# Two additions of a mixing MLP in pieces of one node tile, and another order for the last edge group of a graph layer

## The chip, the cores and the metric

The kernel runs on one core of a Trainium2 chip. The metric is the time of one execution on the device, in microseconds (us). Before the change three runs took 3339.9, 3343.6 and 3344.3 us; their median is 3343.6 us.

In the profile PE is TensorE's matmul part and PEld its weight load, DVE is VectorE, ACT is ScalarE, POOL is GpSimd, SP is SyncE. ACTq and SPq are the queues on which ACT and SP issue DMAs.

## What is computed

One layer over 12,500 nodes of 256 features and 212,500 edges sorted by their destination: a graph attention, a linear attention with an MLP over all nodes (the mixing), and a mixture of experts.

```python
xn = _layernorm(x)
# graph attention, 8 heads of 32
h  = einsum('ni,hif->hnf', xn, W)
ea = leaky(s_src[:, src] + s_dst[:, dst]).T
ea = exp(ea - segment_max(ea, dst)[dst])
ea = ea / (segment_sum(ea, dst)[dst] + EPS)
gnn = segment_sum(hn[src] * ea[:, :, None], dst)      # 12500 x 256
# mixing
y = xn + attention(xn)
h = _layernorm(y, norm_g, norm_b)
mix = y + gelu(h @ w_fc1 + b_fc1) @ w_fc2 + b_fc2
x = x + gnn + mix
return x + ffn(_layernorm(x))                          # top 2 of 8 experts
```

## The kernel before

It is written with one instruction stream for each engine and semaphores between them, in three stages with a barrier between: the node stage (a table with h and the scores of each node is written to HBM), the edge stage, and the stage of routing and experts. The change lies in the edge stage.

**Edges.** 128 edges are a chunk and 16 chunks (`CB`) a group; there are 104 groups (`GROUPS`), the last of them number 103. 212,500 edges fill 1661 chunks; the other three of the 1664 hold padding. For each chunk `edges_pool` issues one indirect DMA on POOL (L1215) that gathers 128 rows of the table into a column of `rows`, by indices that it finds in the SBUF tile `srcix`. `rows` has three buffers (`NR`), so the gather of a chunk waits until the sum of the chunk three groups earlier is made.

A group k then passes through these steps, which the text calls by their functions:

- `copy_scores` (ACT, L1309) waits for all 16 gathers of the group and copies the score columns; `turn_scores` (PE, L1261 and L1262) transposes them into bank 0.
- `breaks` and `edge_scores` (DVE, L1372 to L1409) make the maximum of each segment by scans along the row; `exp_scores` (ACT, L1315) takes the exponential; `turn_weights` (PE, L1268 and L1269) and `copy_weights` (ACT, L1320) turn the result back.
- `one_hot` (DVE, L1381 and L1384) compares each edge's fragment number with a ramp; it makes the matrix that sums the edges of one destination. It needs nothing of the gather. It reads the ramp from bank 0, into which `turn_scores` writes other columns, so the two take turns.
- `weigh` (DVE, L1416, four quarters of a group) multiplies the rows by the weights; `sums` (PE, L1279, four quarters of four chunks, two matmul passes for each chunk) adds up; `copy_sums` (ACT, L1329, a copy for each chunk) moves the sum out of one of three banks. After a group's 16 copies ACT issues two DMAs that store them (L1349, L1351).

The order is written out by hand. On PE `turn_scores(k + 1)` stands ahead of all of `sums(k)`, and `turn_weights(k + 1)` between its second and third quarter. On ACT `exp_scores(k + 1)` and `copy_weights(k + 1)` stand amid `copy_sums(k)`, and `copy_scores(k + 2)` behind it. On DVE `one_hot(k + 1)` stands behind `edge_scores(k + 1)`.

**Beside the edges** run the mixing MLP (in groups up to 91) and most of a merge of fragments across chunks (groups 92 to 101): `Beside` hands out their steps by the count of its calls, four in a group, whatever the time is. `mlp_vector` treats the nodes in 25 supernodes of four tiles of 128 nodes (`SUPERS`; the last has two). Two of its instructions in each supernode add one SBUF tile to another, both 128 partitions by 1024 values: L1154 adds the bias `mb2` to `m_xs`, and L1137 in `ended` adds `m_xs` to the result `m_x2`. The last window of the merge follows the last edge group, then comes the barrier.

Of the kernel before, what the change touches and what calls it, by code (L numbers as in the profile page):

```python
# [33 lines left out]
BLOCKS = -(-GROUPS * CB // P)  # L34
CHUNKS = BLOCKS * P
NEAR = 32
FAR = CHUNKS * NEAR
# [15 lines left out]
NR = 3  # L53
# [1037 lines left out]
def mlp_vector(v, vec, S, B):  # L1091
# [41 lines left out]
    def ended(k):  # L1133
        if k >= 0:
            x2, n = B.m_x2[k % 2], SUPERS[k][1]
            v.wait_ge(S.m_y, pairs_to(k))
            v.tensor_tensor(x2[:, 0:n, :], x2[:, 0:n, :], B.m_xs[:, 0:n, :], ALU.add).then_inc(S.m_x3, 1)  # L1137

# [5 lines left out]
    for k, (s, n) in enumerate(SUPERS):  # L1144
        free = mlp_banks(k)[2]
        added(k - 1, 1)
        yield
        ended(k - 1)
        yield
        yield from idle(3)  # L1150
        attended(k + 1, 0, free)
        yield
        v.wait_ge(S.m_xs, 16 * (k + 1))
        vec(v.tensor_tensor(B.m_xs[:, 0:n, :], B.m_xs[:, 0:n, :], B.mb2[:, :].unsqueeze(1).to_broadcast([P, n, D]), ALU.add))  # L1154
        v.wait_ge(vec.sem, vec.n)
        yield
        yield from idle(2)
        attended(k + 1, 1, free)
        yield
        yield from norm(k + 1)  # L1160
        added(k, 0)
        yield
# [45 lines left out]
def edges_pool(p, S, B, groups):  # L1208
    for k in groups:
        b = k % NR  # L1210
        for j in range(CB):
            col = k * CB + j
            if k >= NR:
                p.wait_ge(S.sum, (k - NR) * CB + j + 1)
            p.indirect_dma_start(out=B.rows[b][:, j, :], out_offset=None, in_=B.table[:, :],  # L1215
                                 in_offset=bass.IndirectOffsetOnAxis(ap=B.srcix[:, col:col + 1], axis=0)).then_inc(S.rows_in[b], 16)
# [37 lines left out]
def edges_tensor(pe, S, B):  # L1254
    beside = Beside(mix_tensor(pe, S, B), mlp_tensor(pe, S, B), merge_tensor(pe, S, B))

    def turn_scores(k):
        pe.wait_ge(S.sce, k + 1)
        pe.wait_ge(S.oh, 2 * k)
        pe.wait_ge(S.inb, k)  # L1260
# [23 lines left out]
    for k in range(GROUPS):  # L1284
        more = k + 1 < GROUPS
        if more:
            turn_scores(k + 1)
        sums(k, 0)
        beside()
        sums(k, 1)  # L1290
        beside()
        if more:
            turn_weights(k + 1)
        sums(k, 2)
        beside()
        sums(k, 3)
        beside()
    for _ in beside.steps:
# [3 lines left out]
def edges_scalar(a, S, B):  # L1302
    beside = Beside(mix_scalar(a, S, B), mlp_scalar(a, S, B), merge_scalar(a, S, B))

    def copy_scores(k):
        r, b = k % NR, k % 2
        a.wait_ge(S.rows_in[r], 16 * CB * (k // NR + 1))
        a.wait_ge(S.tsc, max(k - 1, 0))
# [26 lines left out]
    for k in range(GROUPS):  # L1335
        more = k + 1 < GROUPS
        copy_sums(k, 0)
        beside()
        copy_sums(k, 1)
        if more:  # L1340
            exp_scores(k + 1)
        beside()
        if more:
            copy_weights(k + 1)
        copy_sums(k, 2)
        beside()
        copy_sums(k, 3)
        a.wait_ge(S.ev, CB * (k + 1))
        a.dma_start(B.frag[k * CB * NEAR:(k + 1) * CB * NEAR, :].rearrange("(c l) f -> l c f", l=NEAR),  # L1349
                    B.fout[k % 2][0:NEAR, :, :]).then_inc(S.near[k % 2], 16)  # L1350
        a.dma_start(B.last_d[k * CB:(k + 1) * CB, :], B.fout[k % 2][P - 1:P, :, :]).then_inc(S.near[k % 2], 16)  # L1351
        if k + 2 < GROUPS:
            copy_scores(k + 2)
# [9 lines left out]
def edges_vector(v, vec, S, B):  # L1363
# [13 lines left out]
    def one_hot(k):  # L1377
        b = k % 2
        v.wait_ge(S.inb, k + 1)
        v.wait_ge(S.sum, max(CB * (k - 1), 0))  # L1380
# [42 lines left out]
    for k in range(GROUPS):  # L1423
        more = k + 1 < GROUPS
        weigh(k, 2)
        weigh(k, 3)
        if more:
            breaks(k + 1)
            edge_scores(k + 1)
        beside()  # L1430
        if more:
            one_hot(k + 1)
# [952 lines left out]
```

## Time and profile before

| | |
|---|---|
| three runs | 3339.9, 3343.6, 3344.3 us |
| span of the profiled execution, first to last instruction | 3339.0 us |
| POOL busy over the span | 2259.8 us (68%) |
| gathers L1215 | 1664 of 971 ns in the mean, from 153.7 us to 2275.8 us |
| last edge group's last copy | 2300.8 us |
| first instruction behind the barrier | 2317.3 us |

For the profiled execution no time besides its span is given; the runs lie 0.9 to 5.3 us above that span, their median 4.6 us.

How to read it. A busy share over the whole span mixes three stages. For the edge stage the useful views are those that give, for one engine, the duration of each instruction and the idle time ahead of it. An engine whose instructions follow one another with the same short pause all the way is paced by itself; one that waits for others shows pauses of all lengths. Where the durations of equal instructions differ, the timeline shows what ran beside the long ones. At the end of a stage the timeline alone tells which wait ended last.

### The profile page before, as it was taken

How to read it: one execution, taken by the hardware profiler on the slowest of the kernel's cores; microseconds unless marked ns; L12 is line 12 of the kernel's file. 1: busy time of each engine (PE TensorE's matmuls, PEld its weight loads, DVE VectorE, ACT ScalarE, POOL GpSimd, SP SyncE). 2: the span in 40 equal slices, each digit the busy share in tenths (PEclk: the TensorE clock that was granted, in tenths of full speed). 3: DMA queues.
4: the chain of work that ended last, by engine and by line, in shares of the span. 5: the costliest groups of instructions: out<-in, count | busy, mean ns of one | idle time of the engine just before them, and what ended most of it. 6: DMA issues, size and time to landing. Idle time of an engine off the chain costs nothing.

```text
span 3339.0 us, 42310 instructions
## 1 busy us (share of the span) xinstructions
PE 2671.4 (80%) x11566; PEld 2083.1 (62%) x11566; DVE 2000.5 (60%) x5275; ACT 1555.4 (47%) x3383; POOL 2259.8 (68%) x2203
## 2 busy tenths in 40 slices
PE   8657767888888888888898886564289998899997
PEld 6545555665666666566665664443168787778886
DVE  7445566776777767677676766775546456454221
ACT  5335543554554554455555454333245554444442
POOL 0277777777777777777777777773646677666444
PEclk9879988999999999999999998777589999999998
DMA  8797765665666665666566666555756666666552
GB/s 274 249 288 196 203 178 164 170 174 162 171 177 168 180 166 167 179 168 176 160 169 175 167 168 162 163 154 136 265 132 156 163 160 147 142 135 140 99 90 44
DMA packets 399353, 562.41 MB, mean 168 GB/s; under 512 B 72761, under 2 KB 319567, under 8 KB 398938
## 3 DMA queue, kind: packets, MB, share of 16 engines
q0 software_dynamic: 124848, 299.04, 34.8%
q1 hardware_dynamic: 197033, 171.49, 17.6%
q10 hardware_dynamic: 77161, 88.52, 10.2%
q8 instruction: 99, 1.62, 0.2%
q14 instruction: 212, 1.74, 0.2%
HBM read 403.67 MB, written 170.61 MB: 172 GB/s over the span
## 4 chain that ended last, share of the span: by engine, by line
PE 55%; DMA 14%; POOL 11%; issue 8%; ACT 8%; DVE 4%; ACTq 1%; POOLq 0%; SPq 0%; DVEq 0%
PE bank L1279 21%; DMA rows<-table,srcix 9%; PE bank L1082 7%; PE bank L2169 6%; PE bank L2182 6%; POOL rows L1215 5%; PE bank L1071 4%; DMA out<-x_y,x_dest 3%; POOL sorted_d L1708 3%; POOL out L2254 2%; PE bank L1044 2%; PE bank L592 1%; PE bank L593 1%; PE bank L852 1%; ACT L1315 1%
## 5 line engine op out<-in xcount | busy, mean ns | idle before, releaser
L1215 POOL DMA_INDIRECT rows<-table,srcix x1664 | 1615.2, 971 | 507.3 <-issue 353.9
L1279 PE MATMUL bank<-rows,onehot 128*128 128x272 f32 x3328 | 931.9, 428 | 56.0 <-ACT fout L1329 52.5
L1329 ACT ACTIVATE fout<-bank 128x272 f32<-128x272 f32 x1664 | 641.0, 397 | 577.3 <-PE bank L1279 532.3
L1279 PEld LDWEIGHTS bank<-rows,onehot 128*128 128x128 f32 x3328 | 668.9, 208 | 243.7 <-ACT fout L1329 78.7
L1416 DVE TENSOR_TENSOR rows<-rows,bank 128x1024 f32<-128x1024 f32 x416 | 483.9, 1212 | 183.6 <-ACT rows L1320 183.2
L2254 POOL DMA_INDIRECT out<-x_y,x_dest x210 | 336.7, 1603 | 296.6 <-DMA out<-x_y,x_dest 168.8
L2169 PE MATMUL bank<-x_int,x_w1c 128*128 128x256 f32 x1680 | 392.8, 388 | 18.8 <-ACT x_w1c L2198 9.5
L2182 PE MATMUL bank<-e_w,x_ht 128*128 x1680 | 390.6, 387 | 11.7 <-DVE x_y L2235 8.6
L2169 PEld LDWEIGHTS bank<-x_int,x_w1c 128*128 128x128 f32 x1680 | 326.0, 195 | 68.7 <-issue 22.6
L2182 PEld LDWEIGHTS bank<-e_w,x_ht 128*128 128x128 f32 x1680 | 317.7, 194 | 56.8 <-issue 16.0
L2207 ACT ACTIVATE x_ht<-bank,x_b1c 128x256 f32<-128x256 f32 x420 | 174.4, 471 | 376.6 <-PE bank L2169 376.4
L1071 PE MATMUL bank<-m_hnt,fc_w 128*128 128x512 f32 (+1 forms) x600 | 283.9, 598 | 28.9 <-ACT m_hid L1183 28.9
L1261 PE MATMUL bank<-ident,sc_e 128*128 128x128 f32 x104 | 39.1, 376 | 296.4 <-ACT sc_e L1309 287.5
L1082 PE MATMUL bank<-fc_w,m_hid 128*128 128x256 f32 x1176 | 270.8, 382 | 0.0
L1389 DVE SCALAR_TENSOR_TENSOR g_sdm<-notself,bank 128x128 f32<-128x128 f32 x104 | 29.9, 288 | 387.7 <-PE bank L1262 387.3
L1309 ACT ACTIVATE sc_e<-rows 128x256 f32<-128x256 f32 x104 | 43.3, 416 | 449.7 <-DMA rows<-table,srcix 430.6
L1082 PEld LDWEIGHTS bank<-fc_w,m_hid 128*128 128x128 f32 x1176 | 226.3, 192 | 34.4
L1708 POOL DMA_INDIRECT sorted_d<-e_hn,e_row x196 | 193.5, 987 | 64.9 <-issue 53.9
L1381 DVE TENSOR_TENSOR onehot<-bank,loc 128x2032 f32<-128x2032 f32 x104 | 235.6, 2265 | 0.2
L1261 PEld LDWEIGHTS bank<-ident,sc_e 128*128 128x128 f32 x104 | 16.7, 161 | 337.6 <-ACT sc_e L1309 327.1
L1071 PEld LDWEIGHTS bank<-m_hnt,fc_w 128*128 128x128 f32 x600 | 117.1, 197 | 122.9 <-issue 73.8
L2235 DVE TENSOR_TENSOR x_y<-bank,x_b2c 128x512 f32<-128x512 f32 x105 | 72.3, 689 | 184.8 <-PE bank L2182 184.7
(375 smaller groups left out, 3233.4 us busy)
## 6 DMA issues: line engine op xcount, KB each, us to landing
frag<-fout ACTq DMA_DIRECT2D x104, 544.0 KB
x_in<-sorted_d SPq DMA_DIRECT2D x105, 260.0 KB
rows<-table,srcix POOLq DMA_INDIRECT x1664
x_b2c<-in_L_ffn_b SPq DMA_DIRECT2D x105, 128.0 KB, 3.6
frag<-in_x ACTq DMA_DIRECT2D x1, 13416.0 KB
table<-hr SPq DMA_DIRECT2D x24, 544.0 KB, 4.1
xs<-in_x SPq DMA_DIRECT2D x24, 512.0 KB, 6.0
xg<-in_x SPq DMA_DIRECT2D x24, 512.0 KB, 6.3
```

The costliest lines, as they stand in the source:

```text
L1071: t = pe.matmul(bank[own[m % 2]][:, 0:n * P], B.mw1[:, kk, m * P:(m + 1) * P], B.m_hnt[:, kk, 0:n * P], start=(kk == 0), stop=(kk == KD - 1))
L1082: t = pe.matmul(bank[own[i // 2]][:, i % 2 * D:(i % 2 + 1) * D], B.m_hid[:, m, i * P:(i + 1) * P], B.mw2[:, m, :], start=(m == 0), stop=(m ...
L1215: p.indirect_dma_start(out=B.rows[b][:, j, :], out_offset=None, in_=B.table[:, :], in_offset=bass.IndirectOffsetOnAxis(ap=B.srcix[:, col:c ...
L1279: pe.matmul(B.banks[2 + c % 3][:, 0:ROW], B.onehot[k % 2][:, j, :], B.rows[k % NR][:, j, :], start=True, stop=True).then_inc(S.sum, 1)
L1329: a.activation(B.fout[k % 2][:, j, :], B.banks[2 + c % 3][:, 0:ROW], ACT.Copy).then_inc(S.ev, 1)
L1381: v.tensor_tensor(B.onehot[b][:, :, 0:P - 1], B.banks[0][:, 2 * P:3 * P - 1].unsqueeze(1).to_broadcast([P, CB, P - 1]), B.loc[:, k * CB:(k ...
L1416: v.tensor_tensor(h, h, w.unsqueeze(3).to_broadcast([P, n, GH, GF]), ALU.mult).then_inc(S.wgh, 1)
L1708: p.indirect_dma_start(out=B.sorted_d[:, :], out_offset=bass.IndirectOffsetOnAxis(ap=B.e_row[:, j, at:at + 1], axis=0), in_=B.e_hn[r % NH] ...
L2169: t = pe.matmul(out, B.w1c[u][:, k, m * P:(m + 1) * P], B.gt[u][:, k, :], start=(k == 0), stop=(k == KD - 1))
L2182: t = pe.matmul(bk[BANKS_OUT[u]][:, i * D:(i + 1) * D], B.ht[u][:, m, i * P:(i + 1) * P], B.w2[:, bass.ds(ex * HT + m, 1), :], start=(m == ...
L2207: a.activation(B.ht[u][:, m, :], B.banks[BANKS_H[m * 2 // HT]][:, m % 2 * ET:(m % 2 + 1) * ET], ACT.Gelu, bias=B.b1c[w][:, m:m + 1]).then_ ...
L2254: p.indirect_dma_start(out=B.out[:, :], out_offset=bass.IndirectOffsetOnAxis(ap=B.dest[j % (NOUT + 1)][:, i:i + 1], axis=0), in_=B.y[j % N ...
```

## The change

Three things are changed.

1. The two additions in `mlp_vector` are made a node tile at a time: four instructions of 128 by 256 in place of one of 128 by 1024. In `ended` the last of the four waits until the others are complete, since it alone raises the semaphore `m_x3` that lets the result be stored.
2. The three chunks of padding are not gathered: `edges_pool` issues 1661 gathers, and `copy_scores` of the last group waits for 13.
3. In the iteration of group 102 the work for group 103 is put in another place. On PE `turn_scores(103)` goes behind three quarters of `sums(102)`, and `turn_weights(103)` behind the fourth. On ACT `copy_scores(103)` goes behind two quarters of `copy_sums(102)`, and `exp_scores(103)` and `copy_weights(103)` behind all of it. On DVE `one_hot(103)` goes ahead of `breaks(103)` and `edge_scores(103)`; `turn_scores(103)` now waits for it.

```diff
 def ended(k):
-            v.tensor_tensor(x2[:, 0:n, :], x2[:, 0:n, :], B.m_xs[:, 0:n, :], ALU.add).then_inc(S.m_x3, 1)
+            for i in range(n - 1):
+                vec(v.tensor_tensor(x2[:, i, :], x2[:, i, :], B.m_xs[:, i, :], ALU.add))
+            v.wait_ge(vec.sem, vec.n)
+            v.tensor_tensor(x2[:, n - 1, :], x2[:, n - 1, :], B.m_xs[:, n - 1, :], ALU.add).then_inc(S.m_x3, 1)
...
-        vec(v.tensor_tensor(B.m_xs[:, 0:n, :], B.m_xs[:, 0:n, :], B.mb2[:, :].unsqueeze(1).to_broadcast([P, n, D]), ALU.add))
+        for i in range(n):
+            vec(v.tensor_tensor(B.m_xs[:, i, :], B.m_xs[:, i, :], B.mb2[:, :], ALU.add))
...
 def edges_pool(p, S, B, groups):
-        for j in range(CB):
+        for j in range(min(CB, REAL - k * CB)):          # REAL = -(-N_EDGES // P) = 1661
...
 def edges_tensor: turn_scores(k)
-        pe.wait_ge(S.oh, 2 * k)
+        pe.wait_ge(S.oh, 2 * k + (2 if k == GROUPS - 1 else 0))
 def edges_tensor: the loop
-        more = k + 1 < GROUPS
-        if more:
+        more, early = k + 1 < GROUPS, k + 2 < GROUPS
+        if early:
             turn_scores(k + 1)
         sums(k, 0)
         sums(k, 1)
-        if more:
+        if early:
             turn_weights(k + 1)
         sums(k, 2)
+        if more and not early:
+            turn_scores(k + 1)
         sums(k, 3)
+        if more and not early:
+            turn_weights(k + 1)
 def edges_scalar: copy_scores(k), and the loop
-        a.wait_ge(S.rows_in[r], 16 * CB * (k // NR + 1))
+        a.wait_ge(S.rows_in[r], 16 * (CB * (k // NR) + min(CB, REAL - k * CB)))
...
         copy_sums(k, 1)
-        if more:
+        if early:
             exp_scores(k + 1)
-        if more:
+        if early:
             copy_weights(k + 1)
+        elif more:
+            copy_scores(k + 1)
         copy_sums(k, 2)
         copy_sums(k, 3)
+        if more and not early:
+            exp_scores(k + 1)
+            copy_weights(k + 1)
...
-        if k + 2 < GROUPS:
+        if k + 3 < GROUPS:
             copy_scores(k + 2)
 def edges_vector: one_hot(k), and the loop
-        v.wait_ge(S.inb, k + 1)
+        v.wait_ge(S.inb, min(k + 1, GROUPS - 1))
...
         weigh(k, 3)
+        if more and not early:
+            one_hot(k + 1)
         if more:
             breaks(k + 1)
             edge_scores(k + 1)
-        if more:
+        if early:
             one_hot(k + 1)
```

On DVE in the MLP, at the first supernode, before: `m_x<-m_x,m_xs` is the addition of L1137, between the scores and the one-hot of an edge group.

```order
L1409 TENSOR_TENSOR g_fm<-g_d,neq 128x128
L1137 TENSOR_TENSOR m_x<-m_x,m_xs 128x1024
L1381 TENSOR_TENSOR onehot<-bank,loc 128x16x127
L1384 CAST onehot<-islast 128x16
```

The same place in the changed kernel:

```order
L1423 TENSOR_TENSOR g_fm<-g_d,neq 128x128
L1139 TENSOR_TENSOR m_x<-m_x,m_xs 128x256 x3
L1141 TENSOR_TENSOR m_x<-m_x,m_xs 128x256
L1395 TENSOR_TENSOR onehot<-bank,loc 128x16x127
```

One row became four instructions at the same place of the stream; nothing around it moved.

On ACT at the last edge groups, before. The rows begin with eight copies of group 101; `sc_e<-rows` is `copy_scores(103)`, `g_w<-g_ea` is `exp_scores(103)`, `rows<-bank` is `copy_weights(103)`.

```order
L1329 ACTIVATE fout<-bank 128x272 x8
L1349 DMA frag<-fout 32x16x272
L1351 DMA last_d<-fout 1x4352
L1309 ACTIVATE sc_e<-rows 128x256
L1329 ACTIVATE fout<-bank 128x272 x8
L1315 ACTIVATE g_w<-g_ea 128x128
L1320 ACTIVATE rows<-bank 128x2x16x8
L1329 ACTIVATE fout<-bank 128x272 x8
```

Changed:

```order
L1363 DMA frag<-fout 32x16x272
L1365 DMA last_d<-fout 1x4352
L1338 ACTIVATE fout<-bank 128x272 x8
L1318 ACTIVATE sc_e<-rows 128x256
L1338 ACTIVATE fout<-bank 128x272 x8
L1324 ACTIVATE g_w<-g_ea 128x128
L1329 ACTIVATE rows<-bank 128x2x16x8
L1363 DMA frag<-fout 32x16x272
L1365 DMA last_d<-fout 1x4352
L1338 ACTIVATE fout<-bank 128x272 x16
```

All 16 copies of group 102 are now ahead of `exp_scores(103)`, eight of them ahead of `copy_scores(103)`.

On PE at the same place, before: the first two rows are `turn_scores(103)`, `bank<-ident,g_w` and `bank<-ident,g_fm` are `turn_weights(103)`; `bank<-rows,onehot` are sums, where the listing counts one for each chunk and pass.

```order
L1261 MATMUL bank<-ident,sc_e 128x128
L1262 MATMUL bank<-ident,sc_e 128x128
L1279 MATMUL bank<-rows,onehot 128x272 x8
L1268 MATMUL bank<-ident,g_w 128x128
L1269 MATMUL bank<-ident,g_fm 128x128
L1279 MATMUL bank<-rows,onehot 128x272 x24
```

Changed:

```order
L1284 MATMUL bank<-rows,onehot 128x272 x20
L1266 MATMUL bank<-ident,sc_e 128x128
L1267 MATMUL bank<-ident,sc_e 128x128
L1284 MATMUL bank<-rows,onehot 128x272 x4
L1273 MATMUL bank<-ident,g_w 128x128
L1274 MATMUL bank<-ident,g_fm 128x128
L1284 MATMUL bank<-rows,onehot 128x272 x16
```

The x20 are eight chunks of group 101 and twelve of group 102, which stood behind `turn_scores(103)` before.

## Rows read from the trace of the kernel before

**Rows 1.** The page: the chain that ended last, by engine and by line.

```profile
PE 55%; DMA 14%; POOL 11%; issue 8%; ACT 8%; DVE 4%; ACTq 1%; POOLq 0%; SPq 0%; DVEq 0%
```

**Rows 2.** The page's groups: count, then busy us and mean ns, then idle before.

```profile
L1215 POOL DMA_INDIRECT rows<-table,srcix x1664 | 1615.2, 971 | 507.3 <-issue 353.9
```

**Rows 3.** Instructions of L1215: duration min/median/max in ns, first and last start.

```profile
L1215 POOL DMA_INDIRECT rows<-table,srcix x1664: 942/949/1970, 153.7 to 2274.8; - x185
```

**Rows 4.** Stretches: length, busy us (count) of PE, PEld, DVE, ACT, POOL; PEclk, DMA, GB/s.

```profile
588.00:2045.00 1457.00, 1244.59 (x4895) 911.94 (x4893) 1018.90 (x2188) 758.57 (x1661) 1109.27 (x1141) 0.94 0.61 170
```

**Rows 5.** Instructions of L1137 and of L1154, as in rows 3.

```profile
L1137 DVE TENSOR_TENSOR m_x<-m_x,m_xs x25: 685/1219/1258, 623.9 to 2042.0; 128x1024 f32<-128x1024 f32 x24, 128x512 f32<-128x512 f32 x1
L1154 DVE TENSOR_TENSOR m_xs<-m_xs,fc_b x25: 685/1216/1221, 588.2 to 2004.0; 128x1024 f32<-128x1024 f32 x24, 128x512 f32<-128x512 f32 x1
```

**Rows 6.** Timeline, two places: start, us, engine, line; idle before in brackets.

```profile
623.94 1.22 DVE L1137 TENSOR_TENSOR m_x<-m_x,m_xs 128x1024 f32<-128x1024 f32 x1
...
624.56 1.42 POOL L1215 DMA_INDIRECT rows<-table,srcix  x1 [0.30 <-PE bank L1279]
...
1054.53 1.21 DVE L1154 TENSOR_TENSOR m_xs<-m_xs,fc_b 128x1024 f32<-128x1024 f32 x1
1054.61 1.95 POOL L1215 DMA_INDIRECT rows<-table,srcix  x1 [0.30 <-issue]
```

**Rows 7.** Timeline, in the merge: two additions or products follow each other on DVE.

```profile
2111.01 1.23 DVE L1591 TENSOR_TENSOR mg_last<-mg_last,mg_cbeta 128x1024 f32<-128x1024 f32 x1 [6.24 <-ACT mg_cbeta L1521]
2111.16 1.90 POOL L1215 DMA_INDIRECT rows<-table,srcix  x1 [0.30 <-issue]
2112.15 0.18 DVE L1592 TENSOR_TENSOR mg_last<-mg_last,mg_cbeta 128x32 f32<-128x32 f32 x1
```

**Rows 8.** Instructions of L523 in the node stage, and their timeline.

```profile
L523 DVE TENSOR_TENSOR ix_hot_lo<-wcat,avec x4: 415/416/417, 12.1 to 13.1; 128x256 f32<-128x256 f32 x4
...
12.13 1.42 DVE L523 TENSOR_TENSOR ix_hot_lo<-wcat,avec 128x256 f32<-128x256 f32 x4
```

**Rows 9.** Timeline, the last edge groups (102 and 103).

```profile
2271.17 3.52 ACT L1329 ACTIVATE fout<-bank 128x272 f32<-128x272 f32 x8 [0.17 <-SPq L1248]
...
2272.13 4.60 DVE L1416 TENSOR_TENSOR rows<-rows,bank 128x1024 f32<-128x1024 f32 x4
...
2274.84 0.95 POOL L1215 DMA_INDIRECT rows<-table,srcix  x1 [0.30 <-issue]
...
2275.10 0.36 ACTq L1351 DMA_DIRECT2D last_d<-fout  x1
...
2280.92 0.42 ACT L1309 ACTIVATE sc_e<-rows 128x256 f32<-128x256 f32 x1 [6.22 <-DMA rows<-table,srcix]
...
2281.39 0.48 PE L1261 MATMUL bank<-ident,sc_e 128*128 128x128 f32 x1 [7.13 <-ACT sc_e L1309]
...
2282.19 0.29 DVE L1389 SCALAR_TENSOR_TENSOR g_sdm<-notself,bank 128x128 f32<-128x128 f32 x1 [4.79 <-PE bank L1262]
...
2284.84 0.40 ACT L1329 ACTIVATE fout<-bank 128x272 f32<-128x272 f32 x1 [0.51 <-PE bank L1279]
...
2285.46 0.28 DVE L1409 TENSOR_TENSOR g_fm<-g_d,neq 128x128 f32<-128x128 f32 x1
...
2285.66 2.27 DVE L1381 TENSOR_TENSOR onehot<-bank,loc 128x2032 f32<-128x2032 f32 x1
...
2287.85 0.30 ACT L1315 ACTIVATE g_w<-g_ea 128x128 f32<-128x128 f32 x1
...
2289.10 4.61 DVE L1416 TENSOR_TENSOR rows<-rows,bank 128x1024 f32<-128x1024 f32 x4 [1.08 <-ACT rows L1320]
...
2293.64 0.97 ACT L1329 ACTIVATE fout<-bank 128x272 f32<-128x272 f32 x3 [0.88 <-PE bank L1279]
...
2294.85 5.90 ACT L1329 ACTIVATE fout<-bank 128x272 f32<-128x272 f32 x13 [0.24 <-PE bank L1279]
```

**Rows 10.** A stretch of that end, columns as in rows 4.

```profile
2281.40:2286.00 4.60, 4.60 (x13) 3.60 (x14) 3.54 (x12) 1.47 (x4) 0.00 (x0) 0.55 0.00 0
```

More of the change, by code:

```diff
@@ L35 @@
 CHUNKS = BLOCKS * P
+REAL = -(-N_EDGES // P)
 NEAR = 32
@@ L1335, in edges_scalar @@
     for k in range(GROUPS):
-        more = k + 1 < GROUPS
+        more, early = k + 1 < GROUPS, k + 2 < GROUPS
         copy_sums(k, 0)
@@ L1423, in edges_vector @@
     for k in range(GROUPS):
-        more = k + 1 < GROUPS
+        more, early = k + 1 < GROUPS, k + 2 < GROUPS
         weigh(k, 2)
         weigh(k, 3)
+        if more and not early:
+            one_hot(k + 1)
         if more:
```

## The prediction

> **What bounds the kernel now.** I read four views in this order: the chain that ended last, the page's groups, the instructions of the gather line L1215, and the timeline where its durations differ. The chain names TensorE first (55%) and POOL with 11% [rows 1]. That does not settle it: the chain goes back through whatever released each step, and inside an edge group it runs through TensorE even when the group as a whole came late. The gathers tell more. Their 1664 instructions have 507.3 us of idle time ahead of them [rows 2], which is 0.305 us each, and the timeline shows 0.30 wherever one looks [rows 6, 7, 9]. Half of the instructions take 949 ns or less [rows 3]. So POOL issues one gather each 0.949 + 0.305 = 1.254 us from 153.7 to 2275.8 us and waits for nobody: **the edge stage is paced by POOL**, 1664 x 1.254 = 2086.7 us. TensorE is busy 1244.6 of 1457 us beside the MLP, 85%, and DVE 70% [rows 4]: near, but not full.
>
> The stage lasts longer than 2086.7 us because some gathers take up to 1970 ns [rows 3]. The groups have 1615.2 us busy [rows 2], and 1664 x 0.949 = 1579.1, so stalls inside gathers cost 36.1 us. What stalls them is in the timeline. A gather that starts 0.08 us behind an L1154 lasts 1.95 us, one that starts 0.62 us behind an L1137 lasts 1.42 us [rows 6]. Both end 0.82 us after the DVE instruction ends (1054.53 + 1.21 = 1055.74, the gather at 1056.56; 625.16 and 625.98). An undisturbed gather would have 0.82 us left at 0.949 - 0.82 = 0.13 us past its start. So it asks for something 0.13 us in, and it gets it only when the DVE instruction is over. I followed this for all 50 instructions of the two lines: 1.22 us each [rows 5], and the gathers that ask while they run lose 9.7 us at L1137 and 11.3 us at L1154, together **21.0 us of the 36.1**.
>
> The Trainium skill (SBUF — State Buffer, section Who interferes with whom) has the reason: a VectorE instruction with two SBUF inputs takes a read port that it shares with GpSimd, for its whole length, and blocks a GpSimd instruction that reads SBUF. The trace agrees: the stalls end with the DVE instruction, and the gather reads its indices from `srcix`.
>
> **Part 1: the additions in four pieces.** Let a gather start s after the DVE instruction. In the trace it is stalled for s from about 0.05 us on, by 1.09 - s (1.01 for the 0.08 above, 0.47 for the 0.62). Gathers start every 1.254 us, at any phase, so one instruction costs on average (1.09 - 0.05)^2 / 2 / 1.254 = 0.43 us; 50 of them 21.5, where the trace has 21.0. Now the pieces. A 128x256 product of two SBUF tiles takes 0.416 us, and four in a row 1.42 us [rows 8], one each 0.335. A gather that asks in a piece's time waits until the end of that piece, if POOL is served between two pieces: (0.416 - 0.13 - 0.05)^2 / 2 / 1.254 = 0.022 us for each of 196 pieces (98 node tiles, twice), 4.4 us. Putting the pieces at the 50 recorded places, with the gathers at their recorded phases, gives 5.2 us. I take 5.2, the one with this kernel's phases: **-15.8 us**.
>
> Is POOL served in between? In the merge L1592, also with two SBUF inputs, starts at 2112.15, before L1591 ends at 2112.24; the gather between them ends at 2113.06, which is 0.82 behind L1591 and not 0.82 behind L1592's 2112.33 [rows 7]. All the places of this kind that I found in the merge read so. They are few, which keeps the other answer alive (below). The bounds of this part: no stall left, -21.0; POOL never served inside a chain, the replay gives 33.0 us of stalls, +12.0.
>
> DVE has more to do: (1.42 - 1.22) for L1154, and some 0.3 for L1137, whose last piece waits for the three ahead; 25 x 0.5 = 12.5 us on an engine that is 70% busy [rows 4]. Behind L1137 stand `one_hot` and `weigh`, and PE waits for those; a group comes 0.3 us later in one group of three. No gather waits for it, since none waits for a sum now. I cost it at nothing; without that cover it would be up to 12.5 us.
>
> **Parts 2 and 3: the end of the edge stage.** Three gathers fewer are 3 x 1.254 = 3.8 us on POOL. What becomes of that is decided by the chain behind it, which I follow in the times of rows 9. *Before:* the last gather starts at 2274.84, its data lets `copy_scores(103)` start at 2280.92. Meanwhile PE stands still, for 7.1 us, though group 102's rows were weighted by 2276.7: its sums are queued behind `turn_scores(103)`. They then run at half clock, 1.2 GHz (0.55 granted in that stretch [rows 10]); `exp_scores(103)` waits for eight of their copies until 2287.85, though the scores were ready at 2285.5; `weigh(103)` starts at 2289.10, the first copy of group 103 at 2293.64, and the last is over at 2300.76.
>
> *After:* PE goes on with group 102 as soon as group 101 is summed (its last copy is over at 2274.7), and ACT, free of its DMA issues at 2275.5, makes eight copies (8 in 3.52 us [rows 9]) until 2279.0. By then the 13 gathers have landed (2280.9 - 3.8 = 2277.1), so ACT copies the scores at 2279.0 to 2279.5. PE has to end the third quarter, whose last chunk needs a bank that ACT frees at 2279.9, so the transposes run at about 2280.4. `one_hot(103)`, 2.3 us on DVE behind `weigh(102)`, is over at 2279.1 and `breaks(103)` at 2279.9, ahead of it. `edge_scores(103)` starts at 2281.0, takes its 3.55 us (2282.19 to 2285.74 [rows 9]) to 2284.6, with the difference that `exp_scores` reads ready at 2284.4. ACT has ended group 102 near 2283.5 and starts at once; 1.25 us from there to `weigh(103)` as before (2287.85 to 2289.10) gives 2285.6. One quarter of weighing, 1.2, and a sum later the first copy is at 2287.4. Sixteen copies took 2300.76 - 2293.64 = 7.1 us; the last ends at 2294.5: **6.2 us earlier**, padding included. The two DMA issues of group 102 (0.8 us on ACT, now behind `copy_weights(103)`) lie under `weigh(103)`. With the 3.8 us alone, in the old order, it would be 3.8.
>
> Against it stands the clock. PE has only two transposes to do from about 2283.3 to 2286.8. Before, after 7.1 us with nothing, it was granted half (0.55) for the first 4 us of work, in which a chunk takes 0.9 us instead of 0.44 (the copy at 2284.84 lasts 0.40 and had waited 0.51 for PE [rows 9]). If that comes back, 4 us hold 4.4 chunks instead of 9.1, a loss of 2.1 us. The gap is shorter than the old one, so I take half of it, 1.0, and have **-5.2 us**, between -4.1 and -6.2. If neither the padding nor the reordering brings anything, this part is 0.
>
> **Sum.** -15.8 - 5.2 = -21.0. The profiled span 3339.0 becomes 3318.0. The runs' median lies 4.6 us above that span, so the time is 3343.6 - 21.0 = **3322.6 us**. Everything behind the barrier starts earlier and stays as it is.
>
> **Rivals.**
> *A, slower: POOL is not served inside a chain of pieces.* For it: each piece starts 0.08 us before its predecessor's recorded end (0.335 against 0.416 [rows 8]), so the next may hold the port already, and the witnesses [rows 7] are followed by much shorter instructions. Against it: those same rows. Price: stalls last up to 1.42 us, the replay gives 23.6 us if the wait ahead of L1137's last piece lets POOL in and 33.0 if not, for 21.0 now. With the end's -5.2 the time is 3341.0 to 3350.4. It turns slower than before where a chain stalls by over 26.2 us in all.
> *B: what stalls the gathers is not these instructions but something that comes with them, so their length does not matter.* Then only the end of the stage is left, 3343.6 - 5.2 = 3338.4. Against it: durations of 1.95, 1.42 and 1.90 us, each 0.82 us past the end of a `tensor_tensor` [rows 6, 7]. The same page and section of the Trainium skill says that a `tensor_tensor` was not seen to stall DMAs, and infers that writing descriptors needs only the write port; by that the first part would bring nothing, and the rows disagree.
> *C: something behind POOL takes the gain.* PE at 85% and DVE at 70% of a stretch that gets 1% shorter have room; only if the chain of a group were already as long as three groups of gathers would a gather begin to wait for a sum. The idle time of 0.305 everywhere speaks against it. If half of the first part went this way: 3330.5.
> That the change does not do what it says is excluded by the order of instructions shown above.
>
> **Chances.** Forecast 0.78, A 0.07, B 0.05, C 0.10. The forecast's own range is 3343.6 less 16 to 25 us, and 2 us of scatter on either side for the three runs (they lie 4.4 us apart): 3317 to 3330. Up to 3331 it takes in part of C; A and B stay outside. About what a measurement can tell from no change is 0.2%, 6.7 us: below 3336.9 is faster, above 3350.3 slower. Faster: 0.78 and most of C, 0.86. Within: B, half of A, a little of C, 0.11. Slower: 0.03, the far end of A.
>
> **What the new profile would show.** The gather's maximum falls from 1970 ns; its mean from 971 to about 961; all gathers together 1661 x 0.949 + 20.3 = about 1597 us busy, and the idle time stays 0.305 each (507). A gather near one of the pieces is stalled by at most 0.24 us. The last gather starts near 2255 (2274.8 - 15.8 - 3.8). No idle time of 7 us on PE behind it; from the last gather's start to the end of the last copy 25.9 us become about 24.5. If gathers beside the pieces last 1.6 us and more, A is right; if idle times over 0.4 us appear ahead of them, C. The prediction is wrong also if the last copies come 0.9 us apart throughout (the clock), which costs 7 us.

## The result and the profile after

| | before | after |
|---|---|---|
| median of eight runs each | 3343.5 us | 3324.3 us |
| all runs | 3337.3 to 3355.8 | 3320.7 to 3330.5 |
| span of the profiled execution | 3339.0 | 3320.5 |
| start of the 1661st gather (the last that holds edges) | 2271.1 | 2256.3 |
| from there to the end of the last copy of group 103 | 29.7 | 25.1 |
| from there to the end of the program | 1038.2 | 1039.1 |

The ratio is 0.9945, with a 95% interval from 0.9931 to 0.996: 18 us faster, between 13 and 23. The forecast was 3322.6 us, in a range from 3317 to 3330, or to 3331 with a part of rival C.

The page of the changed kernel: the first line is the chain that ended last by engine, the second the group of the gathers (L1215 is L1220 now).

```profile
PE 56%; DMA 13%; POOL 9%; ACT 8%; issue 7%; DVE 6%; ACTq 1%; SPq 0%; POOLq 0%; DVEq 0%
...
L1220 POOL DMA_INDIRECT rows<-table,srcix x1661 | 1598.0, 962 | 506.1 <-issue 357.7
```

Against [rows 1, 2] the gathers are busy 17.2 us less, 2.8 of it the three that are gone, and the idle time ahead of each is still 0.305 us (506.1 / 1661). So POOL still paces the stage and waits for nobody; the chain's shares hardly tell it, as before.

The instructions of that line and of the additions: duration min/median/max in ns, first and last start.

```profile
L1220 POOL DMA_INDIRECT rows<-table,srcix x1661: 942/947/1982, 153.5 to 2256.3; - x185
...
L1139 DVE TENSOR_TENSOR m_x<-m_x,m_xs x73: 408/417/452, 627.6 to 2029.0; 128x256 f32<-128x256 f32 x73
...
L1141 DVE TENSOR_TENSOR m_x<-m_x,m_xs x25: 424/425/466, 628.7 to 2029.4; 128x256 f32<-128x256 f32 x25
...
L1159 DVE TENSOR_TENSOR m_xs<-m_xs,fc_b x98: 409/417/479, 585.2 to 1992.1; 128x256 f32<-128x256 f32 x98
```

For [rows 5] there are 196 pieces of 0.42 us where 50 instructions of 1.22 us stood. The maximum of the gathers did not fall (1982 ns for the 1970 of [rows 3]): the four longest that are left, 1.77 to 1.98 us, lie in the merge.

The timeline at two additions, DVE and POOL, as [rows 6]:

```profile
1112.74 1.42 DVE L1159 TENSOR_TENSOR m_xs<-m_xs,fc_b 128x256 f32<-128x256 f32 x4
1113.40 1.58 POOL L1220 DMA_INDIRECT rows<-table,srcix  x1 [0.30 <-PE bank L1284]
...
1444.52 1.08 DVE L1139 TENSOR_TENSOR m_x<-m_x,m_xs 128x256 f32<-128x256 f32 x3
1445.01 1.08 POOL L1220 DMA_INDIRECT rows<-table,srcix  x1 [0.30 <-PE bank L1284]
1445.64 0.42 DVE L1141 TENSOR_TENSOR m_x<-m_x,m_xs 128x256 f32<-128x256 f32 x1
```

The lower gather asks at 1445.01 + 0.13 = 1445.14, in the second piece (1444.86 to 1445.27), and ends at 1446.09, 0.82 us behind that piece: stalled by 0.13 us. The upper one asks at 1113.53, in the third piece, which ends at 1113.83. It ends at 1114.98, 0.82 us behind the *fourth* piece (1114.16), and is stalled by 0.63 us, where at most 0.24 was forecast. Both kinds matter below.

Where the 18.5 us between the spans come from: 14.8 from the stretch up to the 1661st gather, 4.6 from the end of the stage, and 0.9 are lost behind it, which is less than the same stretch differs between other kernels below. Of the 14.8, gathers beside the additions lose 7.6 us instead of 21.0 (13.4), gathers elsewhere 14.1 instead of 15.0 (0.9); the other 0.5 are an earlier first gather (0.2) and idle time (0.3).

The end of the stage, where [rows 9] stood: the sums of group 102, then `copy_scores(103)`, `edge_scores(103)` from its first to its last instruction, `exp_scores(103)`, `weigh(103)`, and the copies of group 103.

```profile
2255.66 5.21 PE L1284 MATMUL bank<-rows,onehot 128*128 128x272 f32 x22
...
2261.89 2.27 DVE L1395 TENSOR_TENSOR onehot<-bank,loc 128x2032 f32<-128x2032 f32 x1
...
2264.16 0.41 ACT L1318 ACTIVATE sc_e<-rows 128x256 f32<-128x256 f32 x1
...
2265.99 0.29 DVE L1403 SCALAR_TENSOR_TENSOR g_sdm<-notself,bank 128x128 f32<-128x128 f32 x1 [1.10 <-PE bank L1267]
...
2269.26 0.28 DVE L1423 TENSOR_TENSOR g_fm<-g_d,neq 128x128 f32<-128x128 f32 x1
2269.37 0.31 ACT L1324 ACTIVATE g_w<-g_ea 128x128 f32<-128x128 f32 x1 [1.22 <-DVE g_ea L1421]
...
2270.63 4.61 DVE L1430 TENSOR_TENSOR rows<-rows,bank 128x1024 f32<-128x1024 f32 x4 [1.09 <-ACT rows L1329]
...
2273.29 0.40 ACT L1338 ACTIVATE fout<-bank 128x272 f32<-128x272 f32 x1 [2.70 <-PE bank L1284]
...
2275.03 6.37 ACT L1338 ACTIVATE fout<-bank 128x272 f32<-128x272 f32 x14 [0.51 <-PE bank L1284]
```

PE no longer stands still for 7.1 us behind the last gather; the exponential starts 0.03 us after the scores are ready instead of 2.3 us.

### The profile page after: what moved, and what is told of

It is laid out like the page before. It is cut to its first block, busy times and chain, and to the rows that moved or that the text cites. A ratio compares the mean times of both kernels' runs of the same rounds, so it can differ in the third digit from the quotient of the medians.

```text
span 3320.5 us, 42453 instructions
## 1 busy us (share of the span) xinstructions
PE 2669.9 (80%) x11566; PEld 2081.3 (63%) x11566; DVE 2013.9 (61%) x5421; ACT 1554.9 (47%) x3383; POOL 2242.3 (68%) x2200
## 4 chain that ended last, share of the span: by engine, by line
PE 56%; DMA 13%; POOL 9%; ACT 8%; issue 7%; DVE 6%; ACTq 1%; SPq 0%; POOLq 0%; DVEq 0%
PE bank L1284 21%; DMA rows<-table,srcix 9%; PE bank L1083 7%; PE bank L2185 6%; PE bank L2198 6%; PE bank L1072 5%; POOL rows L1220 5%; DMA out<-x_y,x_dest 2%; POOL sorted_d L1724 2%; PE bank L1045 2%; PE bank L593 1%; PE bank L594 1%; PE bank L853 1%; POOL out L2270 1%; ACT L1324 1%
## 5 line engine op out<-in xcount | busy, mean ns | idle before, releaser
L1220 POOL DMA_INDIRECT rows<-table,srcix x1661 | 1598.0, 962 | 506.1 <-issue 357.7
```

## The experiments

All numbers of a run's profile below are from one execution. "Time" is the median of a kernel's executions, their number in brackets, and behind it the median of the kernel before in the same comparison. "Stalls" is what gathers last beyond 0.949 us; "beside the additions" are those that start while one of the two additions runs. "End" is the time from the start of the 1661st gather to the end of the last copy. Kernels that gather the padding start their last gather 3.8 us behind the 1661st.

| kernel | time, before | last gather starts | all stalls | beside the additions | end |
|---|---|---|---|---|---|
| before | 3343.5 (8) | 2274.8 | 36.0 | 21.0 | 29.7 |
| after | 3324.3 (8), 3343.5 | 2256.3 | 21.7 | 7.6 | 25.1 |
| pieces_only | 3329.8 (6), 3346.7 | 2257.1 | 19.1 | 8.1 | 29.6 |
| end_only | 3343.2 (12), 3346.7 | 2276.9 | 42.1 | 27.3 | 25.3 |
| halves | 3331.5 (1), 3346.7 | 2263.3 | 24.1 | 10.9 | 28.4 |
| one_input | 3327.2 (1), 3346.7 | 2262.9 | 25.1 | 9.2 | 29.8 |
| one_input_slow | 3331.8 (1), 3339.1 | 2263.3 | 25.5 | 8.6 | 29.8 |
| waits_between | 3322.4 (1), 3339.1 | 2250.5 | 16.7 | 4.9 | 26.4 |
| eighths | 3328.3 (1), 3339.1 | 2264.0 | 28.7 | 16.2 | 25.7 |
| merge_too | 3320.2 (6), 3339.1 | 2251.8 | 17.6 | 6.2 | 27.8 |

### Each part alone

`pieces_only` is the kernel before with the lines of the diff in `mlp_vector`, and nothing else:

```diff
+            for i in range(n - 1):
+                vec(v.tensor_tensor(x2[:, i, :], x2[:, i, :], B.m_xs[:, i, :], ALU.add))
...
+        for i in range(n):
+            vec(v.tensor_tensor(B.m_xs[:, i, :], B.m_xs[:, i, :], B.mb2[:, :], ALU.add))
```

> The kernel before with the two additions in pieces of one node tile, and nothing else of the change. Port theory (a gather is stalled only until the end of the two-input DVE instruction that runs when it asks, and POOL paces the stage): the last gather starts 13 to 16 us earlier than 2274.8, the gathers' busy time falls from 1615 to about 1601 us, from the last gather's start to the end of the last copy it stays near 26 us, time 3328 to 3330. Rival A (POOL not served inside a chain): the last gather starts later than 2274.8 by 3 to 12 us, 3346 to 3355. Rival C (something behind POOL takes it): gathers stall less, but idle times over 0.4 us appear ahead of them and the time is above 3335.

Measured: the ratio to the kernel before is 0.9951 (0.9935 to 0.9968), median 3329.8 us where the kernel before has 3346.7 in the same comparison. The last gather starts at 2257.1, 17.7 us earlier, a little more than expected: 12.9 of it are stalls beside the additions, 4.0 stalls elsewhere, which the change does not touch; without those it would be 13.7. The end takes 29.6 us, as before. Its gathers:

```profile
L1219 POOL DMA_INDIRECT rows<-table,srcix x1664: 942/946/1993, 153.2 to 2257.1; - x185
its engine sat idle before it (us, times) until:
  issue: 355.2, 1166
  PE bank L1283: 151.7, 498
```

The idle times sum to 506.9 us, 0.305 each, as before. This speaks in size and place for the port theory (a gather waits for the DVE instruction with two SBUF inputs that runs when it asks); rival A as a whole (later than 2274.8) and rival C (idle times ahead of gathers) fall.

`end_only` has the rest of the change, and the additions whole.

```diff
-            for i in range(n - 1):
-                vec(v.tensor_tensor(x2[:, i, :], x2[:, i, :], B.m_xs[:, i, :], ALU.add))
+            v.tensor_tensor(x2[:, 0:n, :], x2[:, 0:n, :], B.m_xs[:, 0:n, :], ALU.add).then_inc(S.m_x3, 1)
...
+        vec(v.tensor_tensor(B.m_xs[:, 0:n, :], B.m_xs[:, 0:n, :], B.mb2[:, :].unsqueeze(1).to_broadcast([P, n, D]), ALU.add))
```

> The kernel before with 1661 gathers and the new order of the last edge group, the additions whole. Theory: gathers are stalled as before (36 us in all, last gather starts 3.8 us earlier, 2271.1), and from there to the end of the last copy it takes 25.1 us as in the changed kernel, so the end of the edge stage comes about 4.6 us earlier: 3338 to 3340. Rival: the gain of the end is that of fewer stalls or of chance, and the end comes within 1 us of the old place.

Measured: ratio 0.999 (0.9978 to 1.0001), median 3343.2 for 3346.7. The end takes 25.3 us for 29.7, so 4.4 us are gained there. But the last gather, now the 1661st, does not start 3.8 us earlier than that of before, it starts 2.1 us *later*: its additions stall the gathers by 27.3 us, though up to the last groups the program is that of before, which lost 21.0. With whole additions this sum depends on where the gathers happen to stand when an addition starts (their phase), and 6 us between two executions are possible; the four profiles of `pad_only` and `order_only` below, whose additions are whole too, have 18.7, 22.3, 23.5 and 22.7. The expectation missed that; the profiled execution gained at the end what it lost to chance ahead of it. The times alone do not show the gain of the end: the interval reaches past 1.

### Is it the second SBUF input?

`one_input` and `one_input_slow` put at both places an instruction of the same 128x1024 that reads one SBUF tile. `one_input_slow` multiplies by one column and adds another. The bias and the input are left out of the mixing result.

```diff
-            v.tensor_tensor(x2[:, 0:n, :], x2[:, 0:n, :], B.m_xs[:, 0:n, :], ALU.add).then_inc(S.m_x3, 1)
+            v.tensor_scalar(x2[:, 0:n, :], x2[:, 0:n, :], B.mb2[:, 0:1], None, ALU.add).then_inc(S.m_x3, 1)
```

> The kernel before with both additions replaced by a DVE instruction of the same 128x1024 and at the same place that reads only one SBUF tile (it adds a column of the bias instead of the other tile, so the bias and the input are left out of the mixing result). Port theory: it lasts about 1.2 us as before and gathers beside it are not stalled: busy time of the gathers 1615 - 21 = 1594 us, last gather starts near 2254. Rival B (the stall comes with the place or the length, not with the second SBUF input): the same stalls as before, gathers of 1.4 to 1.97 us beside it, last gather near 2275.

> As one_input, but in the form of L241 (two operations with a column for each), which runs at one element a cycle there (0.414 us for 256), so 1.2 us for 1024 with one SBUF input; the bias and the input are again left out of the mixing result. Port theory: no gather beside it is stalled by more than 0.12 us, and the gathers' busy time falls by about 21 us to 1594. Rival B (length or place): stalls up to 1 us as before, about 21 us in all. If it comes out at 0.75 us each as in one_input, it is in the double-speed form again and tells only the law of length once more.

Both missed their aim. The instruction ran faster than the additions, 0.75 us in the first and 0.81 us in the second for the 1.22 of the same 1024 values, so length and inputs changed together.

```profile
L1154 DVE TENSOR_SCALAR m_xs<-m_xs,fc_b x25: 491/747/873, 586.9 to 1992.0; 128x1024 f32<-128x1024 f32 x24, 128x512 f32<-128x512 f32 x1
```

In this faster form it stalls gathers too, as the timeline of `one_input` shows:

```profile
1113.69 0.74 DVE L1154 TENSOR_SCALAR m_xs<-m_xs,fc_b 128x1024 f32<-128x1024 f32 x1
1113.75 1.50 POOL L1215 DMA_INDIRECT rows<-table,srcix  x1 [0.30 <-PE bank L1279]
```

The gather ends at 1115.25, again 0.82 us behind the DVE instruction (1114.43). The two runs cannot tell one input from two. They agree roughly with the law of length: at 0.75 us it gives (0.75 - 0.18)^2 / 2 / 1.254 = 0.13 us each, 6.5 for 50, and at 0.81 us 7.9; gathers that start while the instruction runs lost 9.2 and 8.6 us. The surplus is not explained, but such sums differ by several us between executions (see `end_only`). Another 3.7 and 4.5 us, not in the table's column, were lost by gathers that had started up to 0.47 us ahead of it, at a second place where this form alone holds them (last section).

What they could not tell, the other traces do. `weigh` (L1416, 1.21 us for 1024 values) and `one_hot` (L1381, 2.27 us for 2032) read one operand from SBUF and the other from a bank, at the pace of the additions. Leaving out the first 0.18 us of each instruction, in which the additions stall nobody either, 321 gathers of the kernel before ask while `weigh` runs and 163 while `one_hot` does, and their durations sum to 0.4 us *less* than 0.949 each; one of the 484 lasts over 1.0 us. In `end_only` it is 320 and 164, 1.7 us less, and again one over 1.0. Two instructions of it with the gathers beside them:

```profile
1006.40 4.62 DVE L1426 TENSOR_TENSOR rows<-rows,bank 128x1024 f32<-128x1024 f32 x4 [5.72 <-ACT rows L1325]
1017.07 2.27 DVE L1391 TENSOR_TENSOR onehot<-bank,loc 128x2032 f32<-128x2032 f32 x1
```

```profile
1006.82 0.95 POOL L1216 DMA_INDIRECT rows<-table,srcix  x1 [0.30 <-PE bank L1280]
1008.07 0.95 POOL L1216 DMA_INDIRECT rows<-table,srcix  x1 [0.31 <-PE bank L1280]
1009.32 0.95 POOL L1216 DMA_INDIRECT rows<-table,srcix  x1 [0.30 <-issue]
...
1018.27 0.94 POOL L1216 DMA_INDIRECT rows<-table,srcix  x1 [0.30 <-PE bank L1280]
```

Of the 41 gathers that ask, by the same count, while one of the additions of the kernel before runs, 37 are stalled by over 0.05 us and the sum is 21.0 us. So this is what the second input does, not the length and not being a `tensor_tensor`. Rival B falls. The rule of the Trainium skill on instructions with two SBUF inputs (SBUF — State Buffer, section Who interferes with whom) agrees; its remark that a `tensor_tensor` does not stall DMAs does not hold for a gather that takes its indices from SBUF.

### How long a piece

`halves` has two pieces of 128x512 at each addition, `eighths` eight of 128x128.

```diff
+        for i in range(0, n, 2):                  # halves
+            vec(v.tensor_tensor(B.m_xs[:, i:i + 2, :], B.m_xs[:, i:i + 2, :], B.mb2[:, :].unsqueeze(1).to_broadcast([P, 2, D]), ALU.add))
...
+        for i in range(2 * n):                    # eighths
+            o = slice(i % 2 * P, (i % 2 + 1) * P)
+            vec(v.tensor_tensor(B.m_xs[:, i // 2, o], B.m_xs[:, i // 2, o], B.mb2[:, o], ALU.add))
```

> The kernel before with both additions in two pieces of 128x512 (0.685 us each; the second of L1137 waits for the first). Port theory with service between pieces: a stall of at most 0.51 us, (0.685-0.13-0.05)^2/2/1.254 = 0.10 us a piece, 98 pieces, 10 us for 21 now: the gathers' busy time falls by 11 us to about 1604, the last gather starts near 2264. Rival A: no service between pieces, stalls up to 1.1 us and no gain.

> The changed kernel with pieces of 128x128 (0.29 us each, eight in a row about 1.7 us). Port theory with service at every end: (0.29-0.13-0.05)^2/2/1.254 = 0.005 us a piece, 392 pieces, 2 us in all, instead of 7.6. If service at an end fails as often as in the changed kernel (about 6 of 25 chains), 0.15 us each more. Rival: the shorter the pieces, the rarer the service, and the sum does not fall under 7.6.

Halves: 10.9 us beside the additions for 10 expected, none over 0.49 us. The law holds. Eighths: 16.2 us where 2 to 3 were expected, twice as much as four pieces; the rival of that expectation is right. A place in its timeline, DVE and then POOL:

```profile
993.43 1.69 DVE L1161 TENSOR_TENSOR m_xs<-m_xs,fc_b 128x128 f32<-128x128 f32 x8
```

```profile
993.68 2.26 POOL L1222 DMA_INDIRECT rows<-table,srcix  x1 [0.30 <-issue]
```

The gather asks at 993.81 in the second piece and ends at 995.94, 0.82 us behind the eighth (995.12). Six pieces ended while it waited for the port. In all chains of this kernel a gather stalled by over 0.07 us got the port at one of two moments: at the end of the piece in which it asked, or at the end of the chain, never in between. 13 of 25 chains of the bias have a stall over 0.3 us, and 3 of the other addition, where the wait ahead of the last piece ends the chain after seven. So rival A is right for a part of the gathers, and the shorter the pieces the larger that part.

### A wait behind every piece

```diff
         for i in range(n):
             vec(v.tensor_tensor(B.m_xs[:, i, :], B.m_xs[:, i, :], B.mb2[:, :], ALU.add))
+            v.wait_ge(vec.sem, vec.n)
```

> The changed kernel with a wait behind every piece, so that no piece stands ready behind another. If the stalls of 0.43 and 0.63 us that the changed kernel has at the chain of the bias come from POOL not being served at the end of the third piece, they are gone: none over 0.29 us at either addition, their sum falls from 7.6 to about 5 us. If they come from something else, they stay. Time as the changed kernel within its scatter.

A place in its timeline, DVE and then POOL:

```profile
1696.62 1.79 DVE L1159 TENSOR_TENSOR m_xs<-m_xs,fc_b 128x256 f32<-128x256 f32 x4
```

```profile
1697.62 1.15 POOL L1221 DMA_INDIRECT rows<-table,srcix  x1 [0.30 <-issue]
```

The gather asks at 1697.75 in the third piece and is stalled by 0.20 us, to the end of that piece. Measured: none over 0.21 us, 4.9 us beside the additions for 7.6. The long stalls of the changed kernel (five of 25 chains of the bias, 0.43 to 0.63 us; six in `pieces_only`) came from not being served at the end of the third piece, and a wait takes them away. The last gather starts at 2250.5, 5.8 us earlier, of which this accounts for 2.7. Of the rest 2.3 are stalls elsewhere, most of them in the merge, whose program is the same and whose products (below) happened to cost 1.1 us here for 3.7, and 0.6 an earlier first gather. At 3322.4 us its one time cannot be told from 3324.3.

`merge_too` adds the same for the products of L1591 in the merge:

```diff
-            h = of[:, 0:m, 0:D].rearrange("p b (h f) -> p b h f", f=GF)
-            vec(v.tensor_tensor(h, h, by.unsqueeze(3).to_broadcast([P, m, GH, GF]), ALU.mult))
+            for b in range(m):
+                h = of[:, b, 0:D].rearrange("p (h f) -> p h f", f=GF)
+                vec(v.tensor_tensor(h, h, by[:, b, :].unsqueeze(2).to_broadcast([P, GH, GF]), ALU.mult))
+                v.wait_ge(vec.sem, vec.n)
```

> waits_between, and in the merge the products of L1591 also in pieces of 128x256 with a wait behind each. In the changed kernel four gathers lose 3.7 us there. Port theory: at most 0.29 us at each, so 2.5 to 3 us less, and with the 2.5 of waits_between the time is about 5 us below the changed kernel, 3316 to 3322 on the same footing as its 3324. Rival: DVE, which the merge already holds up, delays the groups by the longer products (0.3 us each, 14 of them), and the gain is lost.

Measured: ratio 0.9939 (0.9923 to 0.9956), median 3320.2 where the kernel before has 3339.1 in the same comparison. The gathers at these products now lose 0.8 us instead of 3.7, but all stalls sum to 17.6 for the 16.7 of `waits_between`, which lost only 1.1 there without this, and the end takes 27.8. The interval covers the changed kernel's 0.9945: that it is better is possible and not shown.

### The two halves of the end

`pad_only` leaves only the padding out, `order_only` has only the new order.

```diff
-        for j in range(CB):                                 # pad_only
+        for j in range(min(CB, REAL - k * CB)):
...
+        if more and not early:                              # order_only
+            turn_scores(k + 1)
         sums(k, 3)
+        if more and not early:
+            turn_weights(k + 1)
```

> The kernel before, only with the three chunks of padding not gathered. From the start of the last real gather (the 1661st) to the end of the last copy the kernel before takes 29.7 us. With the whole 3.8 us gained it is 25.9; if the landing of those gathers was not what the scores waited for, 29.7. I expect 26 to 27.

> The kernel before, only with the new order of the last edge group, padding gathered. From the start of the 1661st gather to the end of the last copy: 29.7 before, 25.1 in the changed kernel. The scores can be copied only 3.8 us later than in the changed kernel, but ACT came to them 2 us after the landing there, so I expect 27 (2.7 us gained). If the order brings nothing without the padding, 29.7.

> Once more the kernel before with only the padding left out; the first try ran on a chip where every kernel took some 3,800 us and gathers waited up to 19.6 us for their turn. From the start of the 1661st gather to the end of the last copy, 29.7 us before (29.6 in pieces_only, 28.4 in halves, whose last groups are the same): 26 to 27 if the scores of the last group wait for the last gather; 28 to 30 if something else holds them.

> Once more the kernel before with only the new order of the last edge group. From the start of the 1661st gather to the end of the last copy: 27 if the order works without the padding as I worked out, 28 to 30 if it brings nothing alone. In the runs with both it was 25.1 and 25.3, in waits_between 26.4 and in merge_too 27.8.

Both tries are inconclusive. In these comparisons the kernel before itself took 3820 and 3776 us, and single gathers waited up to 19.7 us for the sum that frees their buffer, so POOL did not pace the stage there; what the pieces are worth in such a comparison was not run. `pad_only` took 3798 and 3792 us, `order_only` 3822 and 3796; from the 1661st gather to the last copy it was 39.0 and 36.9 in the one, 45.3 and 38.6 in the other. These numbers differ by more between two runs of one kernel than the effect in question.

The steps inside the end tell more. From `copy_scores(103)` on nothing waits for a gather, so what differs there is the order's. In us, for all fourteen profiles (in the last two rows POOL did not pace, so only the columns from the second on compare):

| kernels | 1661st gather to `copy_scores(103)` | to the first sum of group 103 | first to last sum | to the end |
|---|---|---|---|---|
| before | 9.8 | 11.2 | 7.8 | 0.8 |
| after | 7.9 | 7.7 | 8.7 | 0.8 |
| old order, four more with gathers at pace | 8.9 to 10.2 | 10.9 to 11.3 | 7.8 | 0.8 |
| new order, four more with gathers at pace | 7.9 to 9.2 | 7.7 | 8.6 to 10.0 | 0.8 |
| `pad_only`, both | 18.7, 20.8 | 9.6 | 7.8 | 0.8 |
| `order_only`, both | 20.1, 26.4 | 7.7 | 9.9, 10.3 | 0.8 |

From the scores to the first sum the order gains 3.5 us in the changed kernel, and the sums, which now start at half clock, cost 0.9 more: 2.6 of the 4.6 us are the order's. The other 2.0 lie ahead of `copy_scores(103)`, where three gathers fewer and its new place on ACT work together; how those divide stays open.

## Why the prediction was right

**What bounds the stage.** Right: 0.305 us ahead of each gather before, after and in each part alone. The last gather moved by what the stalls lost, and the end of the program with it, but for the up to 7 us by which the stretch behind the edge stage differs between kernels.

**The size of the first part.** -15.8 was forecast; the stalls beside the additions fell by 13.4 in the changed kernel, to 7.6 us for 5.2. The step that was off is "a gather that asks in a piece's time waits until the end of that piece": it holds for both pieces ahead of the third and for L1139, where a wait follows the third piece. It does not hold for five gathers at the bias. Served at the end of the third piece they would have lost 1.2 us together; they lost 2.9, so this is 1.7 us.

A second term was too small as well. The sum let a gather go free that asks within 0.18 us (0.13 + 0.05) of the start of a piece. That holds for an addition that stands alone: in the kernel before, gathers that asked at up to 0.13 us were free, and one at 0.18 was stalled. It does not hold for the third and fourth piece at the bias, which follow the one ahead without a pause. Seven gathers of the changed kernel asked 0.12 to 0.14 us after the start of one of them, and by the end of that piece alone each had lost 0.27 to 0.29 us, 2.0 together. Without these two terms 3.9 us are left of the 7.6, so the phases were kinder than the recorded ones by 1.3 us: by luck the errors show as 2.4 and not as 3.7. Rival A, priced for all chains or none, should have been priced for a share of them. The witness for service was one place in the merge with a long instruction and a short one behind; it is true, and it showed one outcome of two.

**The 21.0 us of before** were taken as a fixed sum. They are one draw: `end_only` had 27.3 with the same additions. The law with gathers at any phase gives 21.5, and the six profiles with whole additions have 18.7 to 27.3, 22.6 in the mean, so the forecast stood near the middle by luck. The scatter of the runs (3337 to 3356) may be in part this; no run shows it.

**DVE's extra work**, costed at nothing: right. DVE is busy 13.4 us more over the program (2013.9 for 2000.5), no gather waited (behind the first, the idle time ahead of one is at most 0.32 us).

**The end.** -5.2 was forecast, -4.6 measured, and the pair was a kind one: the five kernels with the new end have 25.1 to 27.8, 26.1 in the mean, the five with the old 28.4 to 29.8, 29.4 in the mean, a difference of about 3.4 us. Counted from the 1661st gather, the chain was worked out and measured as follows: `copy_scores(103)` 7.9 and 7.85, `edge_scores(103)` 9.9 and 9.7, `exp_scores(103)` 13.3 and 13.1, `weigh(103)` 14.5 and 14.3, the last copy 23.4 and 25.1. All steps held but the last. There the clock did come back to half: the stretch from `weigh(103)` on, against [rows 10] (columns as in rows 4),

```profile
2265.00:2270.00 5.00, 2.98 (x15) 2.12 (x14) 3.27 (x11) 2.85 (x8) 0.00 (x0) 1.00 0.00 0
2270.00:2276.00 6.00, 4.27 (x14) 3.18 (x13) 5.30 (x8) 1.97 (x5) 0.00 (x0) 0.72 0.45 96
2276.00:2282.00 6.00, 4.96 (x22) 3.76 (x20) 0.57 (x6) 4.71 (x12) 0.00 (x0) 1.00 0.00 0
```

0.72 is half clock (1.2 GHz) for about 3.4 of the 6 us, granted after PE had had nothing but two transposes from 2267.7 to 2271.9. The last step took 10.8 us for the 8.9 worked out at full clock, and the chain ended 1.7 us later than worked out, where the sum had 1.0 for the clock.

**Behind the barrier** nothing was forecast to change; 0.9 us more were measured, and the same stretch differs by up to 7 us between the kernels of the table (1020 to 1028 us behind the barrier).

**The sum.** The span was forecast at 3318.0 and came to 3320.5, 2.5 us more: 2.4 in the first part, 0.6 at the end and 0.9 behind it, less the 1.4 by which stalls elsewhere, the first gather and idle time happened to be smaller. The time missed by 1.7 us only, since the median lies 3.8 us above the profiled span and the sum took the 4.6 of the kernel before. The mechanism is shown; that the number came so close is in part luck.

## What to carry to other kernels

Before shortening or moving an instruction, ask which engine's instructions follow one another with a constant pause: that one paces, and what makes its instructions longer goes into the time of the stage. A DVE instruction with two SBUF operands beside a POOL queue full of gathers cost about the square of its length less 0.18 us, over twice the gathers' pitch, so cutting it in pieces paid; a wait between the pieces took away the long stalls that were left (a gain in time is not shown for it), since without one the next piece can keep the port, and very short pieces kept it more often than the four of this change. In a hand-written order the last round deserves an order of its own: nothing is behind it that the steady order was made for.

## What the runs showed of the hardware

- A gather of 128 rows behaves as if it asked for the port 0.13 us after its start and needed 0.82 us from there. In the kernel before and in the changed one, all stalls over 0.02 us of gathers that asked while an addition ran hold to that within 0.01 us.
- A gather that is not served at the end of the piece in which it asked is not served at any later end inside the chain: with eight pieces of 0.28 us it was stalled by up to 1.31 us. Why it is passed over is not known. In the changed kernel and `pieces_only` it happened at the third of four pieces for gathers that had asked 0.79 us or about 0.99 us into the chain, and not for those that asked at 0.82 or 1.03.
- `tensor_scalar` of 32-bit values from SBUF to SBUF ran at 0.75 us for 1024 values with one column and 0.81 us with two, and held gathers at a second place as well: gathers that had begun 0.16 to 0.47 us ahead of it ended 0.12 us behind its end, or 0.16 us for the latest of them. The additions with two inputs did not do that.
